# Attention in pairs of slots, with one batch of value products per pair, and maxima split before they are turned

## The chip, the cores and the metric

The kernel runs on one core of one Trainium2 chip. The time is that of the device in microseconds, from launch to end on that core. The kernel before took 1920.18 us in the median of three runs (1919.38 to 1920.65). The profiled execution is one further run.

## The reference

One pre-norm layer over x of 2 x 2048 tokens by 256: attention with 16 heads of 16 channels, then a feed-forward block with ternary weights.

```python
q, k, v = proj(Wq, bq), proj(Wk, bk), proj(Wv, bv)        # of layernorm(x)
scores = einsum('bhqd,bhkd->bhqk', q, k) / sqrt(16)
dp = clip(decay_params, 0.01, 0.9999)
mask = sum over 2 decays of softmax(mix_weights) * dp ** abs(t_q - t_k)
probs = softmax(scores * mask, axis=-1)                   # 2048 x 2048 for each batch and head
x = x + (probs @ v) @ Wo.T + bo
x = x + relu(layernorm(x) @ Wq1.T + b1) @ Wq2.T + b2      # Wq1, Wq2 are ternary: -1, 0, 1
```

No part of the 2048 x 2048 scores is skipped, and the maximum of each row is taken exactly, before the exponentials.

## The kernel before

Three blocks run one after another: a token block (norm, projections, tables of decay powers), the attention block, which is most of the time, and the feed-forward block. The change is in the attention block alone.

**Steps, units, slots.** The attention block makes 16 steps (8 pairs of heads in 2 batches). A step has two heads and 32 slots. Eight slots are a unit: one head and one half (1024) of its queries, so there are four units in a step. A slot handles two blocks of 128 keys. For each of them TensorE makes a tile of scores of 128 keys by 1024 queries (`scores`, L1054 to L1073), ScalarE makes its exponentials (L936), and TensorE multiplies them with the values into the bank `acc` (`products`, L1075 to L1089).

**Levels.** The decay is handled by levels: q and k come multiplied with powers of the decay for blocks of 1024, 512, 256 and 128, each as a sum of two fp16 parts (`hi`, `lo`), stacked in `q_stack` and `k_stack`. The block on the diagonal is taken from the raw q and k (the fifth level) times a mask. In half of the slots of a unit each tile has one such diagonal block, added by a transpose (L1066), in the other half none: "slots with a diagonal" and "slots without" below.

**Maxima.** A softmax needs the maximum of a row before its exponentials. So 12 slots ahead (`LEAD`) TensorE makes the scores once more, of 128 queries by 2048 keys (`max_scores`, L1018 to L1044). They pass through `ring`, three PSUM banks of 512 columns, in four items to a slot. VectorE reduces the items 0, 1 and 2 (L963), and of item 3 first 384 columns (L965) and then the 128 of the diagonal with the mask (L967). TensorE may write an item once VectorE has given back the bank that was filled three items earlier (`ring_free`). After a unit's last block VectorE reduces the parts to `row_max` (L976), ScalarE repeats it (L916), TensorE turns it into the ring (`turn_max`, L1052), VectorE splits it into two fp16 rows (L985, L987, L990), and SyncE stores these into `q_stack` (L776), whence they enter the next unit's scores as two more rows.

**Building the next pair.** During step i GpSimd multiplies q and k of the next pair with the powers (L157), ScalarE casts the product to `hi` (L165), and GpSimd subtracts for `lo` (L171), in 10 chunks (`CHUNKS`). Chunks 0 and 1 are the raw level, straight from `qk`. `cast` of chunk 0 waits for `qk_in` (the loads of `builder.load`, six DMAs) and for `raw_in` of both heads (the copies of the raw level of the build before, which read `hi` and `lo`).

**What sets the order.** All orders are written out by hand, each engine does its own in turn, and semaphores join them. SyncE issues the DMAs in one fixed order with waits between: in the third unit of a step it waits for the split maxima (L776), then issues `builder.load` of the pair after next (L117, L119, four at L125), a mask (L770), the six raw copies of head 1 (L752), and a store. ScalarE's casts of the next pair stand at the slots in `hi_slot`, chunk 0 at slot 0 of the step.

## Time and profile before

| | before |
|---|---|
| median of three runs | 1920.18 us |
| profiled execution | 1918.94 us |
| its span, first to last instruction | 1917.1 us |
| TensorE busy | 1795.7 us (94%) |
| VectorE busy | 1589.5 us (83%) |
| ScalarE busy | 1326.7 us (69%) |
| GpSimd busy | 812.1 us (42%) |
| mean granted TensorE clock | 0.969 |

An engine's instructions overlap their neighbours by their pipelines, so "busy" counts more than what an instruction holds up: the distance from one start to the next is what the argument uses. A granted clock of 1.00 is 2.4 GHz, 0.50 is 1.2 GHz. Times in a row are from the start of the span.

### The profile page before, as it was taken

The page shows a single profiled execution, that of the slowest core. Times are in us where ns is not written, and L with a number is a line of the kernel's source. Part 1 is how long each engine was busy: PE and PEld are TensorE (multiplying, and loading weights), DVE is VectorE, ACT ScalarE, POOL GpSimd, SP SyncE. Part 2 cuts the span into 40 slices and gives each one's busy share as a digit, 9 for nine tenths or more (in the row PEclk, how much of TensorE's full clock was granted, in tenths as well). Part 3 has the DMA queues.
Part 4 walks back from the last instruction along what each step waited for, and adds up shares of the span by engine and source line. Part 5 has one row for each costly group of instructions (what it writes and reads, how often), then busy time and mean ns, then how long its engine had stood idle before and what let it go on. Part 6 is the DMA issues. An engine that isn't in the chain of part 4 may idle for free. (4 is left out here: it accounts for less than half of the span.)

```text
span 1917.1 us, 32073 instructions
## 1 busy us (share of the span) xinstructions
PE 1795.7 (94%) x11794; PEld 749.4 (39%) x11794; DVE 1589.5 (83%) x3756; ACT 1326.7 (69%) x1526; POOL 812.1 (42%) x409
## 2 busy tenths in 40 slices
PE   3856999999999999999999999999999999995998
PEld 2521333333333333333333333333333333324666
DVE  7866888888888888888888888888888888835785
ACT  2343868686868686868686868686868686673555
POOL 6340908081818181818181818171727272002010
PEclk9875999999999999999999999999999999996999
DMA  6988363636363636363636363636363634207531
GB/s 156 267 270 192 75 154 91 154 90 155 91 155 90 154 91 154 94 154 94 154 94 154 93 154 94 154 94 153 93 154 93 154 94 110 67 18 187 146 91 34
DMA packets 132442, 242.62 MB, mean 127 GB/s; under 512 B 27696, under 2 KB 62896, under 8 KB 122032
## 3 DMA queue, kind: packets, MB, share of 16 engines
q1 hardware_dynamic: 129376, 237.84, 51.1%
q0 software_dynamic: 560, 2.36, 1.2%
q8 instruction: 92, 1.51, 0.3%
q10 hardware_dynamic: 2352, 0.40, 0.1%
q14 instruction: 62, 0.51, 0.1%
HBM read 69.08 MB, written 44.56 MB: 59 GB/s over the span
## 5 line engine op out<-in xcount | busy, mean ns | idle before, releaser
L936 ACT ACTIVATE probs<-tile 128x1024 f32<-128x1024 f32 x1024 | 999.5, 1024 | 297.8 <-PE tile L1066 170.0
L963 DVE TENSOR_REDUCE part_max<-ring 128x1 f32<-128x512 f32 x1536 | 964.0, 682 | 183.2 <-PE ring L1038 183.2
L1038 PE MATMUL ring<-k_stack,q_stack 96*128 96x512 f16 (+2 forms) x3072 | 661.1, 314 | 27.6 <-DMA q_stack<-lo 18.0
L1069 PE MATMUL tile<-q_stack,k_stack 98*128 98x512 f16 (+2 forms) x2560 | 588.6, 328 | 9.5 <-ACT probs L936 9.1
L1085 PE MATMUL acc<-probs,v_ones 128*32 128x512 f32 x4096 | 546.1, 605 | 0.0
L1069 PEld LDWEIGHTS tile<-q_stack,k_stack 98*128 98x128 f16 x2560 | 211.3, 98 | 575.5 <-ACT probs L936 346.7
L873 POOL TENSOR_TENSOR diag<-diag,row_max 128x1024 f32<-128x1024 f32 x64 | 121.4, 1897 | 643.1 <-DVE row_max L976 643.1
L1038 PEld LDWEIGHTS ring<-k_stack,q_stack 96*128 96x128 f16 x3072 | 262.6, 99 | 312.7 <-DVE part_max L963 178.9
L157 POOL TENSOR_TENSOR decayed<-qk,table_in 128x1024 f32<-128x1024 f32 x128 | 305.3, 2391 | 59.7 <-DMA table_in<-table_scratch 46.8
L965 DVE TENSOR_REDUCE part_max<-ring 128x1 f32<-128x384 f32 x512 | 278.8, 545 | 7.5 <-PE ring L1038 7.5
L171 POOL TENSOR_TENSOR lo<-decayed,hi 128x1024 f16<-128x1024 f32 x120 | 256.3, 2136 | 10.1 <-ACT hi L165 10.1
L165 ACT CAST hi<-decayed 128x1024 f16<-128x1024 f32 x128 | 134.3, 1049 | 61.1 <-POOL decayed L157 61.0
L967 DVE CUSTOM_DVE_ANT_0 diag<-ring,mask 128x128 f32<-128x128 f32 x512 | 143.3, 280 | 2.0
L1066 PE MATMUL tile<-ident,diag 128*128 128x128 f32 x512 | 142.8, 279 | 0.0
L171 POOL TENSOR_TENSOR lo<-qk,hi 128x1024 f16<-128x1024 f32 x30 | 64.1, 2137 | 178.2 <-ACT hi L165 178.2
L1085 PEld LDWEIGHTS acc<-probs,v_ones 128*32 128x32 f32 x4096 | 80.8, 108 | 57.0 <-issue 3.0
L1323 ACT ACTIVATE h_hi<-up,b_col 128x512 f16<-128x512 f32 x64 | 43.9, 685 | 54.4 <-PE up L1470 53.8
L1398 DVE TENSOR_TENSOR h_lo<-hidden,h_hi 128x512 f16<-128x512 f32 x64 | 50.1, 782 | 32.0 <-ACT hidden L1324 31.4
L1066 PEld LDWEIGHTS tile<-ident,diag 128*128 128x128 f32 x512 | 71.6, 140 | 6.2
L1284 POOL TENSOR_TENSOR x_bias<-x_res,bo_all 128x1024 f32<-128x1024 f32 x8 | 18.8, 2349 | 119.8 <-DVE y L1367 103.5
L927 ACT COPY heads_out<-acc 128x512 f32<-128x512 f32 x64 | 37.5, 586 | 22.3 <-PE acc L1085 22.3
L567 PE MATMUL turn<-ident,x_tokens 128*128 128x128 f32 x64 | 10.5, 318 | 39.3 <-DVE x_tokens L79 39.3
(145 smaller groups left out, 1041.1 us busy)
## 6 DMA issues: line engine op xcount, KB each, us to landing
q_stack<-hi SPq DMA_DIRECT2D x320, 128.0 KB, 3.8
k_stack<-hi SPq DMA_DIRECT2D x128, 256.0 KB, 4.3
q_stack<-lo SPq DMA_DIRECT2D x160, 128.0 KB, 3.0
table_in<-table_scratch SPq DMA_DIRECT2D x64, 256.0 KB, 8.3
k_stack<-lo SPq DMA_DIRECT2D x64, 256.0 KB, 3.7
out_scratch<-heads_out SPq DMA_DIRECT2D x64, 256.0 KB, 3.1
v_scratch<-v_out SPq DMA_DIRECT2D x8, 1024.0 KB, 6.5
q_scratch<-q_out SPq DMA_DIRECT2D x32, 256.0 KB, 3.8
```

Of the source, the lines that this page charges most:

```text
L157: self.nc.gpsimd.tensor_tensor(self.source(c), self.half_view(self.qk[:], level, side), self.factors(level, side), ALU.mult).then_inc(self ...
L165: self.nc.scalar.copy(self.half_view(self.hi[:, level], level, side), self.source(c)).then_inc(self.hi_ready, 1)
L171: ops.tensor_tensor(self.half_view(self.lo[:, level], level, side), self.source(c), self.half_view(self.hi[:, level], level, side), ALU.su ...
L873: nc.gpsimd.tensor_tensor(part, part, row_max[:, half].unsqueeze(2).broadcast_to([P, UNIT_SLOTS, P]), ALU.subtract).then_inc(diag_ready, 1)
L936: nc.scalar.activation(probs[:, t % 4], tile[t % 2][:].rearrange("p a b -> p (a b)"), ACT.Exp, scale=1.0 / (SCALE * SCALE * HEAD_DIM ** 0. ...
L963: nc.vector.tensor_reduce(out[:, k:k + 1], ring_bank(n), AX.X, ALU.max).then_inc(ring_free, 1)
L965: nc.vector.tensor_reduce(out[:, 3:4], ring_bank(n)[:, 0:3 * P], AX.X, ALU.max).then_inc(blocks_seen, 1)
L967: nc.vector.tensor_tensor_reduce(out=diag[h][:, q], in0=ring_bank(n)[:, 3 * P:4 * P], in1=mask[h][:], scale=1.0, scalar=-3.0e38, op0=ALU.m ...
L1038: last = nc.tensor.matmul(ring[:, n % RING, col:col + width], q_stack[h][0:STACK, q // UNIT_SLOTS, level, q0:q0 + P], k_stack[h][0:STACK, ...
L1066: last = nc.tensor.matmul(out, diag[h][:, kb], ident[:], is_transpose=True, start=bank not in started, stop=True, skip_group_check=True)
L1069: last = nc.tensor.matmul(out, k_stack[h][:, level, kb * P:(kb + 1) * P], q_stack[h][:, half, level, col:col + width], start=bank not in s ...
L1085: last = nc.tensor.matmul(acc[row:row + ROWS], v_ones[h][:, t % BLOCKS], probs[:, t % 4, qt * 512:(qt + 1) * 512], start=(j % UNIT_SLOTS = ...
```

## The change

- **Pairs of slots.** TensorE goes through slots two by two. The eight products (two slots' tiles) stand together at the end of the pair, after all scores and ring items of both; before, four stood at the end of each slot, for the tiles of the slot before. Item 0 of the ring comes ahead of the pair's first scores.
- **Maxima.** VectorE splits the maxima into two fp16 parts while they are 8 columns wide (`max_parts`); ScalarE repeats both; TensorE turns them by a matmul with the fp16 identity after the products of the pair of slots 4 and 5; VectorE copies them once (`take_max`). `finish_max` comes at slot 3 of a unit instead of slot 4. SyncE waits for `ring_free` of that item.
- **Casts.** One cast to a pair of slots, behind its four exponentials. Chunks 0 and 1 (raw) of the build after next are cast already at slots 25 and 27 of the step, and GpSimd's `begin` does the first four of its steps at the end of the step. SyncE's order of DMAs is the same.
- The copy of `acc` (`take_unit`) stands ahead of the unit's first exponential instead of behind the second.

```diff
@@ -625,7 +625,7 @@
-RED_SLOT, TURN_SLOT = 4, 5
+RED_SLOT, TURN_SLOT = 3, 5
...
+def turn_taken(slot, more, o):
+
+    return RING_STEP * o + turn_item(slot, more) + AHEAD_ITEMS + 1
 
 
...
+        max_parts = sb("max_parts", [P, MAXROWS, UNIT_SLOTS], F16)
+        max_repeated = sb("max_repeated", [P, MAXROWS, RAW, UNIT_SLOTS], F16)
         max_rows = sb("max_rows", [MAXROWS * RAW * UNIT_SLOTS, P], F16)
-        scrap = sb("scrap", [UNIT_SLOTS, 1])
...
-        order = [("rest", 0), ("rest", 1), ("product", 2)]
-        for c in range(3, CHUNKS):
+        order = [("rest", 2)]
+        for c in range(4, CHUNKS):
             order += [("product", c), ("rest", c - 1)]
         order.append(("rest", CHUNKS - 1))
-        pool_steps = (order[:5], order[5:14], order[14:], [])
-        hi_slot = (0, 1, 3, 4, 6, 7, 9, 10, 13, 15)
+        pool_steps = (order[:3], order[3:11], order[11:], [])
+        cast_slot = {2 * c - 3: c for c in range(2, CHUNKS)}
+        raw_slot = {SLOTS - 7: 0, SLOTS - 5: 1}
 
         @block.sync
...
-            def store_max_rows(h, half, count):
-
-                sp.wait_ge(rows_ready, count)
+            def store_max_rows(h, half, taken):
+
+                sp.wait_ge(ring_free, taken)
                 sp.dma_start(q_stack[h][STACK:STACK + MAXROWS, half, 0:RAW],
                              max_rows[:]).then_inc(rows_in, QUADS)
...
-                store_max_rows(1, 1, UNITS * i + 4)
+                store_max_rows(1, 1, turn_taken(2 * UNIT_SLOTS + TURN_SLOT, more, o))
...
+            def begin(builds):
+                for c in range(2):
+                    builder.rest(pool, nc.gpsimd, c, builds)
+                for c in range(2, 4):
+                    free(c, builds)
+                    builder.multiply(c)
+
             pool.sem_inc(diag_ready, 1)
             diag_minus_max(0, 0, 1)
+            begin(1)
             def step(i, o, more):
...
                     diag_minus_max((u // 2) % 2, u % 2, UNITS * i + u + 1)
+                if i + 2 < STEPS:
+                    begin(i + 2)
 
             for_steps(step)
...
 
-            def repeat_max(par, count):
-
-                act.wait_ge(max_ready, count)
-                nc.scalar.copy(max_repeated[:], row_max[:, par].unsqueeze(1).broadcast_to([P, MAXROWS * RAW, UNIT_SLOTS])
+            def repeat_max(count):
+
+                act.wait_ge(parts_ready, count)
+                nc.scalar.copy(max_repeated[:], max_parts[:].unsqueeze(2).broadcast_to([P, MAXROWS, RAW, UNIT_SLOTS])
                                ).then_inc(repeated_ready, 1)
 
 
...
+                    if s % UNIT_SLOTS == 0 and (s > 0 or o > 0):
+                        take_unit(s // UNIT_SLOTS - 1)
                     act.wait_ge(probs_used, SLOTS * o + s + 1)
                     for t in (2 * s, 2 * s + 1):
-                        u = s // UNIT_SLOTS + 1
-                        if s % UNIT_SLOTS == TURN_SLOT and t % 2 and (more or u < UNITS):
-                            repeat_max(u % 2, UNITS * i + u + 1)
                         act.wait_ge(tile_full, EXPS * o + t + 1)
                         nc.scalar.activation(probs[:, t % 4], tile[t % 2][:].rearrange("p a b -> p (a b)"), ACT.Exp,
                                              scale=1.0 / (SCALE * SCALE * HEAD_DIM ** 0.5)).then_inc(exp_done, 1)
-                    if s % UNIT_SLOTS == 0 and (s > 0 or o > 0):
-                        take_unit(s // UNIT_SLOTS - 1)
-                    for c in range(CHUNKS):
-                        if more and hi_slot[c] == s:
-                            cast(c, i + 1)
+                    if more and s in cast_slot:
+                        cast(cast_slot[s], i + 1)
+                    if i + 2 < STEPS and s in raw_slot:
+                        cast(raw_slot[s], i + 2)
+                    u = s // UNIT_SLOTS + 1
+                    if s % UNIT_SLOTS == RED_SLOT and (more or u < UNITS):
+                        repeat_max(UNITS * i + u + 1)
                 if o == STEPS - 1:
                     take_unit(UNITS - 1)
...
 
-            def finish_max(par, seen, count):
-
-                dve.wait_ge(blocks_seen, seen)
-                if count is not None:
-                    dve.wait_ge(diag_ready, count)
+            def finish_max(par, slot, unit, o=0):
+
+                dve.wait_ge(ring_free, RING_STEP * o + ring_item(slot, ITEMS - 1) + AHEAD_ITEMS + 1)
+                if unit >= 1:
+                    dve.wait_ge(diag_ready, unit)
                 nc.vector.tensor_reduce(row_max[:, par], part_max[:, par], AX.X, ALU.max).then_inc(max_ready, 1)
-
-            def split_max(slot, unit_count, more=True, o=0):
+                dve.wait_ge(max_ready, unit + 1)
+                if unit >= 1:
+                    dve.wait_ge(repeated_ready, unit)
+                nc.vector.tensor_scalar(max_parts[:, 0], row_max[:, par], -1.0 / MAXUNIT, None, ALU.mult
+                                        ).then_inc(high_ready, 1)
+                dve.wait_ge(high_ready, unit + 1)
+                nc.vector.scalar_tensor_tensor(out=max_parts[:, 1], in0=row_max[:, par], scalar=-1.0 / MAXUNIT,
+                                               in1=max_parts[:, 0], op0=ALU.mult,
+                                               op1=ALU.subtract).then_inc(parts_ready, 1)
+
+            def take_max(slot, unit_count, more=True, o=0):
 
                 n = turn_item(slot, more)
                 dve.wait_ge(ring_full, RING_STEP * o + n + AHEAD_ITEMS + 1)
                 if unit_count is not None:
                     dve.wait_ge(rows_in, QUADS * unit_count)
-                src = ring_bank(n)[0:MAXROWS * LO_ROWS, 0:P]
-                nc.vector.tensor_scalar(max_rows[:], src, -1.0 / MAXUNIT, None, ALU.mult).then_inc(max_seen, 1)
-                dve.wait_ge(max_seen, (unit_count if unit_count is not None else 0) + 1)
-                nc.vector.scalar_tensor_tensor(out=max_rows[LO_ROWS:], in0=src[LO_ROWS:], scalar=-1.0 / MAXUNIT,
-                                               in1=max_rows[LO_ROWS:], op0=ALU.mult,
-                                               op1=ALU.subtract).then_inc(rows_ready, 1)
-                nc.vector.tensor_copy(scrap[:], src[0:UNIT_SLOTS, 0:1]).then_inc(ring_free, 1)
+                nc.vector.tensor_copy(max_rows[:], ring_bank(n)[0:MAXROWS * LO_ROWS, 0:P]).then_inc(ring_free, 1)
 
             nc.vector.memset(unit[:], MAXUNIT).then_inc(unit_ready, 1)
             for s in range(-LEAD, 0):
                 max_block(s, s + LEAD, 0)
...
-                nc.tensor.transpose(ring[0:MAXROWS * LO_ROWS, n % RING, 0:P],
-                                    max_repeated[:].rearrange("p r b -> p (r b)"), ident[:]).then_inc(ring_full, 1)
+                nc.tensor.matmul(ring[0:MAXROWS * LO_ROWS, n % RING, 0:P], max_repeated[:].rearrange("p m r b -> p (m r b)"),
+                                 keep["ident16"][:], start=True, stop=True, skip_group_check=True).then_inc(ring_full, 1)
 
...
                 max_scores(s, s + LEAD, range(ITEMS), 0)
-                if s % UNIT_SLOTS == TURN_SLOT and s + LEAD >= UNIT_SLOTS:
+                if s == TURN_SLOT - UNIT_SLOTS:
                     turn_max(s, 1)
             pe.wait_ge(const_ready, 2)
             def step(i, o, more):
-                for s in range(SLOTS):
-                    ahead = more or s + LEAD < SLOTS
+                def ahead(s, ks):
+                    if more or s + LEAD < SLOTS:
+                        max_scores(s, s + LEAD, ks, i, o)
+
+                for s in range(0, SLOTS, 2):
                     if s % UNIT_SLOTS == 0:
                         u = s // UNIT_SLOTS
                         pe.wait_ge(rows_in, QUADS * (UNITS * i + u + 1))
                         pe.wait_ge(diag_ready, UNITS * i + u + 2)
+                    ahead(s, (0,))
                     scores(2 * s, o)
-                    if ahead:
-                        max_scores(s, s + LEAD, (0, 1), i, o)
+                    ahead(s, (1,))
                     scores(2 * s + 1, o)
-                    if s == SLOTS - 1 and o == STEPS - 1:
-                        products(s - 1, o)
-                    if ahead:
-                        max_scores(s, s + LEAD, (2, 3), i, o)
-                    j = s if s == SLOTS - 1 and o == STEPS - 1 else s - 1
-                    if j < 0 and o > 0:
-                        products(SLOTS - 1, o - 1)
-                    if j >= 0:
-                        if j % UNIT_SLOTS == 0:
-                            pe.wait_ge(acc_free, UNITS * i + j // UNIT_SLOTS + 1)
-                        if j % (2 * UNIT_SLOTS) == 0:
-                            pe.wait_ge(v_in[j // (2 * UNIT_SLOTS)], QUADS * (i + 1))
-                        products(j, o)
-                    if s % UNIT_SLOTS == TURN_SLOT and (more or s + UNIT_SLOTS < SLOTS):
-                        turn_max(s, UNITS * i + s // UNIT_SLOTS + 2, more, o)
+                    ahead(s, (2, 3))
+                    scores(2 * s + 2, o)
+                    ahead(s + 1, (0, 1))
+                    scores(2 * s + 3, o)
+                    ahead(s + 1, (2, 3))
+                    if s % UNIT_SLOTS == 0:
+                        pe.wait_ge(acc_free, UNITS * i + s // UNIT_SLOTS + 1)
+                    if s % (2 * UNIT_SLOTS) == 0:
+                        pe.wait_ge(v_in[s // (2 * UNIT_SLOTS)], QUADS * (i + 1))
+                    products(s, o)
+                    products(s + 1, o)
+                    if s % UNIT_SLOTS == TURN_SLOT - 1 and (more or s + UNIT_SLOTS < SLOTS):
+                        turn_max(s + 1, UNITS * i + s // UNIT_SLOTS + 2, more, o)
 
             for_steps(step)
```

On TensorE, slots without a diagonal in the first step, before: `tile` are scores of the tile that is exponentiated, `ring` the items for the maxima, `acc` the products with the values.

```order
L1069 MATMUL tile<-q_stack,k_stack 128x512 x2
L1038 MATMUL ring<-k_stack,q_stack 128x512 x2
L1069 MATMUL tile<-q_stack,k_stack 128x512 x2
L1038 MATMUL ring<-k_stack,q_stack 128x512
L1038 MATMUL ring<-k_stack,q_stack 128x256
L1038 MATMUL ring<-k_stack,q_stack 128x128 x2
L1085 MATMUL acc<-probs,v_ones 32x512 x4
L1069 MATMUL tile<-q_stack,k_stack 128x512 x2
L1038 MATMUL ring<-k_stack,q_stack 128x512 x2
L1069 MATMUL tile<-q_stack,k_stack 128x512 x2
```

The same slots after; ahead of the first row stand the eight products of the pair before, one `ring` item, two `tile` rows and one `ring` item.

```order
L1088 MATMUL tile<-q_stack,k_stack 128x512 x2
L1057 MATMUL ring<-k_stack,q_stack 128x512
L1057 MATMUL ring<-k_stack,q_stack 128x256
L1057 MATMUL ring<-k_stack,q_stack 128x128 x2
L1088 MATMUL tile<-q_stack,k_stack 128x512 x2
L1057 MATMUL ring<-k_stack,q_stack 128x512 x2
L1088 MATMUL tile<-q_stack,k_stack 128x512 x2
L1057 MATMUL ring<-k_stack,q_stack 128x512
L1057 MATMUL ring<-k_stack,q_stack 128x256
L1057 MATMUL ring<-k_stack,q_stack 128x128 x2
L1104 MATMUL acc<-probs,v_ones 32x512 x8
```

The products moved from behind every fourth ring item to behind every eighth.

On ScalarE, the start of the fourth unit of the first step (slots 24 to 27), before, from the copy of `acc` on, which here stands behind two exponentials:

```order
L927 COPY heads_out<-acc 128x512 [waits out_stored0,acc_full]
L936 ACTIVATE probs<-tile 128x1024 [waits tile_full,probs_used]
L936 ACTIVATE probs<-tile 128x1024 [waits tile_full]
L936 ACTIVATE probs<-tile 128x1024 [waits tile_full,probs_used]
L936 ACTIVATE probs<-tile 128x1024 [waits tile_full]
L936 ACTIVATE probs<-tile 128x1024 [waits tile_full,probs_used]
L936 ACTIVATE probs<-tile 128x1024 [waits tile_full]
```

The same place after:

```order
L946 COPY heads_out<-acc 128x512 [waits out_stored0,acc_full]
L954 ACTIVATE probs<-tile 128x1024 [waits tile_full,probs_used]
L954 ACTIVATE probs<-tile 128x1024 [waits tile_full]
L954 ACTIVATE probs<-tile 128x1024 [waits tile_full,probs_used]
L954 ACTIVATE probs<-tile 128x1024 [waits tile_full]
L165 CAST hi<-qk 128x1024 [waits raw_in1,raw_in0,qk_in]
L954 ACTIVATE probs<-tile 128x1024 [waits tile_full,probs_used]
L954 ACTIVATE probs<-tile 128x1024 [waits tile_full]
L954 ACTIVATE probs<-tile 128x1024 [waits tile_full,probs_used]
L954 ACTIVATE probs<-tile 128x1024 [waits tile_full]
L165 CAST hi<-qk 128x1024
```

Two casts that stood in the next step moved here, and the first waits for three semaphores of DMAs.

## Rows read from the trace of the kernel before

**Rows 1.** The stretches view of one whole step: engines' busy us, clock, DMA.

```profile
313.10:409.50 96.40, 95.76 (x646) 36.37 (x644) 84.76 (x208) 73.61 (x84) 47.41 (x23) 1.00 0.53 123
```

**Rows 2.** The timeline, ScalarE, one step apart: start us, us, engine, line.

```profile
313.08 0.58 ACT L927 COPY heads_out<-acc 128x512 f32<-128x512 f32 x1
...
409.46 0.59 ACT L927 COPY heads_out<-acc 128x512 f32<-128x512 f32 x1
```

**Rows 3.** The timeline, TensorE, two slots without a diagonal and one with.

```profile
797.13 0.60 PE L1069 MATMUL tile<-q_stack,k_stack 98*128 98x512 f16 x2
...
800.06 0.61 PE L1069 MATMUL tile<-q_stack,k_stack 98*128 98x512 f16 x2
800.50 0.60 PE L1038 MATMUL ring<-k_stack,q_stack 96*128 96x512 f16 x2
...
803.25 0.56 PE L1069 MATMUL tile<-q_stack,k_stack 98*128 98x512 f16 x3 [0.19 <-ACT probs L936]
...
805.24 1.07 PE L1085 MATMUL acc<-probs,v_ones 128*32 128x512 f32 x8
```

**Rows 4.** The same in narrow windows: rests of item 3, next scores, a turn.

```profile
801.67 0.40 PE L1038 MATMUL ring<-k_stack,q_stack 96*128 96x256 f16 x3
...
804.92 0.40 PE L1038 MATMUL ring<-k_stack,q_stack 96*128 96x256 f16 x3
...
806.24 0.50 PE L1069 MATMUL tile<-q_stack,k_stack 98*128 98x512 f16 x2
...
809.24 0.30 PE L1052 MATMUL ring<-ident,max_repeated 128*64 128x128 f32 x1
809.37 0.38 PE L1069 MATMUL tile<-q_stack,k_stack 98*128 98x512 f16 x1
```

**Rows 5.** TensorE in the last slots of the attention, products of two slots in turn.

```profile
1719.11 1.06 PE L1085 MATMUL acc<-probs,v_ones 128*32 128x512 f32 x8
...
1719.99 1.83 PE L1085 MATMUL acc<-probs,v_ones 128*32 128x512 f32 x8
```

**Rows 6.** The timeline, VectorE: one slot's four items, and a split.

```profile
800.92 1.89 DVE L963 TENSOR_REDUCE part_max<-ring 128x1 f32<-128x512 f32 x3 [0.37 <-PE ring L1038]
802.72 0.55 DVE L965 TENSOR_REDUCE part_max<-ring 128x1 f32<-128x384 f32 x1
803.19 0.28 DVE L967 CUSTOM_DVE_ANT_0 diag<-ring,mask 128x128 f32<-128x128 f32 x1
...
809.64 0.28 DVE L985 TENSOR_SCALAR max_rows<-ring 64x128 f16<-64x128 f32 x1
```

**Rows 7.** The timeline, ScalarE: a cast that waited, and four exponentials.

```profile
801.22 1.04 ACT L165 CAST hi<-decayed 128x1024 f16<-128x1024 f32 x1 [1.08 <-POOL decayed L157]
802.17 3.78 ACT L936 ACTIVATE probs<-tile 128x1024 f32<-128x1024 f32 x4
```

**Rows 8.** The timeline, SyncE: from the store of maxima to the last raw copy.

```profile
352.42 0.57 SPq L776 DMA_DIRECT2D q_stack<-max_rows  x1
...
360.70 0.59 SPq L752 DMA_DIRECT2D k_stack<-hi  x1
```

**Rows 9.** DMA issues (KB each, median us to landing), first 353.0 to 361.2, then 314 to 322.

```profile
k_stack<-hi SPq DMA_DIRECT2D x2, 128.0 KB, 8.2
...
q_stack<-hi SPq DMA_DIRECT2D x2, 128.0 KB, 2.4
```

**Rows 10.** The stretches view, TensorE alone: busy us (instructions), clock, DMA share, GB/s.

```profile
26.00:28.00 2.00, 0.48 (x5) 1.00 0.02 4
28.00:30.00 2.00, 0.00 (x0) 1.00 0.00 0
30.00:32.00 2.00, 1.52 (x10) 0.89 1.29 131
32.00:34.00 2.00, 2.00 (x6) 0.50 0.17 9
34.00:36.00 2.00, 2.00 (x9) 0.75 0.95 219
```

More of the change, by code:

```diff
@@ L705, in attention_block @@
         blocks_seen = sem("blocks_seen")
-        max_ready, max_seen = sem("max_ready"), sem("max_seen")
+        max_ready, high_ready, parts_ready = sem("max_ready"), sem("high_ready"), sem("parts_ready")
         repeated_ready = sem("repeated_ready")
-        rows_ready, rows_in = sem("rows_ready"), sem("rows_in")
+        rows_in = sem("rows_in")
         diag_ready = sem("diag_ready")
@@ L800, in _ @@
             builder.load(sp, 1)
-            store_max_rows(0, 0, 1)
+            store_max_rows(0, 0, turn_taken(TURN_SLOT - UNIT_SLOTS, True, 0))
             def step(i, o, more):
@@ L812, in step @@
                     store_out(i - 1, UNITS - 1)
-                store_max_rows(0, 1, UNITS * i + 2)
+                store_max_rows(0, 1, turn_taken(TURN_SLOT, more, o))
                 if more:
@@ L822, in step @@
                     load_q(0, 0, 0)
-                store_max_rows(1, 0, UNITS * i + 3)
+                store_max_rows(1, 0, turn_taken(UNIT_SLOTS + TURN_SLOT, more, o))
                 if more:
@@ L846, in step @@
                         load_q(1, 0, x)
-                    store_max_rows(0, 0, UNITS * i + 5)
+                    store_max_rows(0, 0, turn_taken(3 * UNIT_SLOTS + TURN_SLOT, more, o))
                 if o == STEPS - 1:
@@ L911, in _ @@
                                ).then_inc(const_ready, 1)
-            def repeat_max(par, count):
-                act.wait_ge(max_ready, count)
-                nc.scalar.copy(max_repeated[:], row_max[:, par].unsqueeze(1).broadcast_to([P, MAXROWS * RAW, UNIT_SLOTS])
+            def repeat_max(count):
+                act.wait_ge(parts_ready, count)
+                nc.scalar.copy(max_repeated[:], max_parts[:].unsqueeze(2).broadcast_to([P, MAXROWS, RAW, UNIT_SLOTS])
                                ).then_inc(repeated_ready, 1)
             nc.scalar.activation(warm[:], ident[:, 0:1], ACT.Exp)
-            repeat_max(0, 1)
+            repeat_max(1)
             act.sem_inc(exp_done, 2)
+            for c in range(2):
+                cast(c, 1)
             def step(i, o, more):
@@ L994, in _ @@
                 max_block(s, s + LEAD, 0)
-                if s % UNIT_SLOTS == RED_SLOT and s + LEAD >= UNIT_SLOTS:
-                    finish_max(0, s + LEAD + 1, None)
-                if s % UNIT_SLOTS == TURN_SLOT and s + LEAD >= UNIT_SLOTS:
-                    split_max(s, None)
+                if s == RED_SLOT - UNIT_SLOTS:
+                    finish_max(0, s, 0)
+                if s == TURN_SLOT - UNIT_SLOTS:
+                    take_max(s, None)
             def step(i, o, more):
@@ L1006, in step @@
                     if s % UNIT_SLOTS == RED_SLOT:
-                        seen = SLOTS * i + s + LEAD + 1
-                        if not more and s + LEAD >= SLOTS:
-                            dve.wait_ge(ring_free, RING_STEP * o + ring_item(SLOTS - LEAD - 1, ITEMS - 1) + AHEAD_ITEMS + 1)
-                            seen = SLOTS * STEPS
-                        finish_max(u % 2, seen, UNITS * i + u)
+                        finish_max(u % 2, s, UNITS * i + u, o)
                     if s % UNIT_SLOTS == TURN_SLOT:
-                        split_max(s, UNITS * i + u, more, o)
+                        take_max(s, UNITS * i + u, more, o)
             for_steps(step)
@@ L1096, in _ @@
                 max_scores(s, s + LEAD, range(ITEMS), 0)
-                if s % UNIT_SLOTS == TURN_SLOT and s + LEAD >= UNIT_SLOTS:
+                if s == TURN_SLOT - UNIT_SLOTS:
                     turn_max(s, 1)
```

1 line of the change is left out of this document (removed).

## The prediction

> **What bounds the kernel now.** I looked first at the busy times of one whole step [rows 1]: TensorE 95.8 of 96.4 us, VectorE 84.8, ScalarE 73.6, at the full clock. A step is 409.46 - 313.08 = 96.4 us [rows 2], and the 16 of them are 1542 of the 1917 us. Then TensorE's timeline: a slot without a diagonal takes 800.06 - 797.13 = 2.93 us, one with a diagonal 806.24 - 803.25 = 2.99 [rows 3, 4]. Sixteen of each make 94.7; four turns at 809.37 - 809.24 = 0.13 [rows 4] make 0.5; the other 1.2 us come from casts that wait for GpSimd and hold ScalarE up: the slot that begins at 800.06 takes 3.19 instead of 2.93 [rows 3], since a cast sat waiting in it [rows 7]. So TensorE is the bound, and the reader should see in VectorE's rows that it is close behind: the three reduces of a slot start 0.60 apart (802.72 - 800.92 for three), item 3 costs 0.47 + 0.28, together 2.55 us, and then it idles 0.37 [rows 6].
>
> **What the merged batch removes.** Going into the products costs time: item 3's last 512 columns start at 804.92 and the products at 805.24, 0.32 us [rows 3, 4], where 512 columns take 0.22 (1024 took 800.50 - 800.06 = 0.44) [rows 3]; 0.10 is the way in. Coming out costs too: eight product records last 806.24 - 805.24 = 1.00 us when scores follow [rows 3, 4], but 1719.99 - 1719.11 = 0.88 when products follow [rows 5]; 0.12 is the way out. One way in and out less per pair is 0.22 us, times 256 pairs 56 us. If TensorE stayed the bound, this would be the gain, and more (rivals).
>
> **What it adds: VectorE starves at each batch.** The ring has three banks. The last item 3 of a pair needs the bank of that slot's item 0. VectorE begins the three reduces at 800.92 and ends the first at 801.52, and TensorE starts item 3 at 801.67 [rows 4, 6]: 0.15 from VectorE's end to TensorE's start. From that start: 0.32 to the products, 0.88 + 1.00 for the batch, then item 0 of the next pair, which VectorE can read 0.42 after it starts (800.50 to 800.92) [rows 3, 6]. That is 2.62, plus the 0.15 before it 2.77 us, in which VectorE has the items 1, 2 and 3 left: 0.60 + 0.60 + 0.75 = 1.95. It idles 0.8 us per pair, whatever TensorE saves elsewhere, as long as item 3 is the one that waits. In the new order it is: single ring items lie between scores at the head of the pair, so VectorE also idles between items 0, 1 and 2. These start 0.22 + 0.44 = 0.66 apart without a diagonal and about 0.71 with one, where VectorE takes 0.60: 0.1 and 0.2 us per pair. VectorE's pair is then 2 x 2.55 + 0.8 + 0.1 or 0.2, 6.0 or 6.1 us, against TensorE's 5.86 and 5.98 before. The eight pairs of each kind make 8 x 12.1 = 97.0 us in a step. That the bound passes to VectorE is the whole price; the 56 us are spent in waiting for the ring.
>
> **Maxima.** The split now works on 8 columns: two small operations behind the row reduce, each with a wait for the one before. They lie at the end of the pair of slots 2 and 3, in VectorE's 0.8 us of idleness, and cost nothing; if that cover were gone, at most 0.6 us, twice the 0.28 of today's split, four times per step. The copy of 64x128 should take the 0.28 of the split of the same shape [rows 6]; it and the 0.13 of the turn fall at the head of a pair, partly over one another: 0.13 to 0.28, I take 0.2, four times per step 0.8. A step is 97.8 without the casts.
>
> **Casts 2 to 9.** They come behind a pair's four exponentials. ScalarE has 4 x 0.92 + 0.95 = 4.6 us [rows 7] of work in 6.0, and GpSimd begins earlier, so the 1.2 us of cast stalls go; that is already in the 97.8. So far: 97.8 - 96.4 = +1.4 us, times 16 steps +22 us (bounds: 0 and +45, by 0.1 us less or more per pair). GpSimd's four steps ahead and the copy of `acc` before the exponentials lie in idle time: GpSimd is busy 47 of 96 us, ScalarE 74 [rows 1].
>
> **The raw cast at slot 25.** This is the largest term. ScalarE works in order; the cast of chunk 0 there waits for DMAs that SyncE issues in the same unit. SyncE's order is unchanged: the last raw copy is issued 360.70 - 352.42 = 8.3 us after the store of the maxima and lands 8.2 us after that [rows 8, 9], so 16.5 after the store. The store comes later now: the turn stands at the end of the pair of slots 20 and 21, and with 0.42 for VectorE to see it, 0.28 for the copy and about 0.05 it is issued 0.8 us into the pair of 22 and 23, that is 5.3 us before the products of that pair are done. The raw level is thus in 11.2 us into the pair of 24 and 25. ScalarE is through the copy of `acc` and four exponentials about 0.35 + 0.6 + 0.2 + 4 x 0.92 = 4.8 us into it. It waits 6.4 us, casts in 0.95, and the exponential that was due at 6.0 + 1.2 = 7.2 starts at 12.1: 5 us late. TensorE has two tiles and can fill the ring, then waits for that exponential; nothing after it is ahead of time, so all 5 us are lost. It happens in the 14 steps with a build after next: 70 us. By bounds, 3 and 6.5 us a step (raw level landing 2 us sooner or 1.5 later): 42 and 91.
>
> The Trainium skill ("DMA: Bandwidth & Descriptors", on the two cost components) fits a DMA's time as about 2.0 us fixed plus its bytes at 436 GB/s. By that fit, as an estimate, the raw copies would land some 2.3 us after issue and the wait would be half a us. The same copy does land in 2.4 us where the queue is empty [rows 9]. Behind the six loads of the builder it took 8.2, so the trace speaks against the fit here; that it might hold is rival B.
>
> **The clock.** TensorE stands still about 5 us in each of these waits. In the token block it stood 0.48 us busy in 26 to 28, then not at all to about 30.5, 4.0 us; thereafter the granted clock was 0.89, 0.50 and 0.75 in three stretches of 2 us, which is 0.4 + 2.0 + 1.0 = 3.4 us at 1.2 GHz [rows 10]. Half of that is lost where TensorE is the bound: 1.7 us, times 14 = 24 us (bounds 0 and 35).
>
> The Trainium skill ("TensorE: Matmul & The Clock Gate", Part 1) holds that the cost of ramping is below 1% of a typical kernel's span; taken as an estimate, that is at most 19 us here where my term is 24, and the sum would be 2030.
>
> **The sum.** 1918.9 of the profiled execution (0.07% under the median of 1920.2) + 22 + 70 + 24 = 2035 us.
>
> **Rivals.** A: all as above, but the clock stays up, since items of the ring still run now and then in the wait: 2011. For it: the wait is interrupted by two tiles' scores at its start; against: the row above.
> B: the raw level is there when slot 25's exponentials end. Then the cast fits ScalarE's idle time: 1918.9 + 22 = 1941. Against: [rows 9] and SyncE's fixed order.
> C, the other side: VectorE doesn't starve and TensorE remains the bound. The pair would be 2 x 2.93 - 0.22 less the 0.08 per slot that item 3 waits now (item 3 starts at 801.67, where 800.50 + 0.44 + 0.44 + 0.22 = 801.60 was open to it), 5.48, and with a diagonal 5.98 - 0.22 - 0.04 = 5.72; a step 8 x 11.2 + 0.5 = 90.1 us, 6.3 less, 100 us in all: 1819. It decides from VectorE's idle time at a batch below 0.3 us instead of 0.8, which needs a ring that is given back sooner than rows 4 and 6 show. With the raw cast's wait of 5.6 us as well (78, and 24 for the clock) it is 1819 + 78 + 24 = 1921: the same.
> D: only part of the raw cast's wait reaches TensorE (half): 1918.9 + 22 + 35 + 12 = 1988.
>
> **How the numbers follow.** Forecast 0.57, A 0.17, B 0.09, D 0.08, C without the cast's wait 0.04, with it 0.03, anything else slower 0.02. Forecast's own range by the terms' bounds: 2005 to 2060. For 8 in 10 the range holds the forecast, A and the upper part of D: 1992 to 2058. A measurement of this kernel tells 0.2% (4 us) from no change: faster 0.04, same 0.03, slower 0.93.
>
> **What would show it.** Right: in the timeline products x16 records per pair and pairs 6.0 and 6.1 us long; VectorE idle 0.8 us before the first reduce of each pair; TensorE's weight loads waiting for `part_max` more than today; on ScalarE an idle time of some 6 us before the cast of `qk` at slot 25, ended by a DMA to a stack or `qk`; steps of 104 to 105 us in the first 14 and 98 in the last ones; a clock of 0.5 for about 3 us after each wait. Wrong: steps all alike (B); pairs under 5.8 us (C); a clock of 1.00 through the waits (A). The forecast falls if the store of the maxima in the third unit comes several us earlier than I placed it, or if the loads of the builder land sooner.

## The result and the profile after

The changed kernel takes 2224.8 us (median of four runs, 2223.8 to 2227.4), the kernel before 1920.4 in the same comparison: a ratio of 1.159 (95% interval 1.157 to 1.160). The forecast of 2035 had the sign right and missed 190 of the 304 us; its range ended at 2058.

The first rows of the page after (busy us, share of the span, instructions) tell where not to look. TensorE and VectorE are "busy" longer than before, on as many instructions, and yet by a smaller share of the span: both wait.

```profile
span 2223.8 us, 32136 instructions
PE 1903.8 (86%) x11794; PEld 826.8 (37%) x11794; DVE 1761.7 (79%) x3756; ACT 1322.6 (59%) x1526; POOL 812.3 (37%) x409
```

A step takes 113.9 to 118.3 us, mostly 116 (before 96.4 [rows 2], forecast 104 to 105). What the forecast had named is there. On ScalarE's timeline, the fourth unit of a step begins with the copy of `acc`; then come four exponentials, and the raw cast waits 6.25 us for a DMA (forecast 6.4). This place is one of the shorter of the 14: they range from 6.1 to 7.8 us, 6.9 in the mean.

```profile
977.17 0.59 ACT L946 COPY heads_out<-acc 128x512 f32<-128x512 f32 x1 [1.40 <-PE acc L1104]
977.93 3.77 ACT L954 ACTIVATE probs<-tile 128x1024 f32<-128x1024 f32 x4 [0.17 <-PE tile L1088]
987.95 1.04 ACT L165 CAST hi<-qk 128x1024 f16<-128x1024 f32 x1 [6.25 <-DMA k_stack<-hi]
```

SyncE had stored the maxima 16.4 us before that cast, and issued the last raw copy 8.3 us after them, as in [rows 8]:

```profile
971.50 0.58 SPq L782 DMA_DIRECT2D q_stack<-max_rows  x1
...
979.80 0.60 SPq L758 DMA_DIRECT2D k_stack<-hi  x1
```

TensorE stands still for 5.1 us in it; over the 14 waits it is 5.0 to 6.7 us, 5.8 in the mean (forecast 5).

```profile
984.26 0.60 PE L1057 MATMUL ring<-k_stack,q_stack 96*128 96x512 f16 x4
989.98 1.04 PE L1088 MATMUL tile<-q_stack,k_stack 98*128 98x512 f16 x2 [5.12 <-ACT probs L954]
```

The stretches view of TensorE there (length, busy us and instructions, granted clock, DMA share, GB/s) answers to [rows 10]: the clock goes to 1.2 GHz and is back at 2.4 by 996, so that some 6 us of work are done at half speed, against the 3.4 that the term had.

```profile
986.00:988.00 2.00, 0.00 (x0) 1.00 1.01 288
988.00:990.00 2.00, 0.02 (x1) 0.79 1.09 244
990.00:992.00 2.00, 2.00 (x5) 0.50 0.39 79
992.00:994.00 2.00, 2.00 (x10) 0.50 0.00 0
994.00:996.00 2.00, 2.00 (x12) 0.50 0.04 8
996.00:998.00 2.00, 2.00 (x18) 1.00 0.00 0
```

The surprise is in the groups of instructions by form (busy us, mean ns of one, idle before): the two operations on 8 columns, costed at nothing, take 1.76 and 1.06 us in the mean. The reduce ahead of them, on 40 columns, takes 0.20.

```profile
L1003 DVE SCALAR_TENSOR_TENSOR max_parts<-row_max,max_parts 128x8 f16<-128x8 f32 x64 | 112.6, 1759 | 2.2
L1000 DVE TENSOR_SCALAR max_parts<-row_max 128x8 f16<-128x8 f32 x64 | 67.6, 1057 | 2.4 <-DVE row_max L996 0.2
...
L996 DVE TENSOR_REDUCE row_max<-part_max 128x8 f32<-128x40 f32 x64 | 12.5, 195 | 2.2
```

VectorE's timeline of one such place, in the second unit of a step (start, us):

```profile
904.99 0.20 DVE L996 TENSOR_REDUCE row_max<-part_max 128x8 f32<-128x40 f32 x1
905.22 1.98 DVE L1000 TENSOR_SCALAR max_parts<-row_max 128x8 f16<-128x8 f32 x1
907.23 1.81 DVE L1003 SCALAR_TENSOR_TENSOR max_parts<-row_max,max_parts 128x8 f16<-128x8 f32 x1
908.96 0.68 DVE L983 TENSOR_REDUCE part_max<-ring 128x1 f32<-128x512 f32 x1
```

And GpSimd's at the same time:

```profile
905.04 2.12 POOL L171 TENSOR_TENSOR lo<-decayed,hi 128x1024 f16<-128x1024 f32 x1 [0.29 <-ACT hi L165]
907.12 1.89 POOL L879 TENSOR_TENSOR diag<-diag,row_max 128x1024 f32<-128x1024 f32 x1
```

The reader should lay the ends beside each other. GpSimd's first instruction ends at 907.16, VectorE's first at 907.20; GpSimd's second at 909.01, VectorE's second at 909.04. VectorE's operation ends when GpSimd's has. TensorE then waits for a bank of the ring:

```profile
909.70 0.39 PE L1057 MATMUL ring<-k_stack,q_stack 96*128 96x256 f16 x3 [2.68 <-DVE part_max L983]
```

The second operation meets the subtraction `diag_minus_max` (L879), which the same reduce releases: 63 of the 64 begin inside a GpSimd instruction, take 1.75 to 1.82 us and end 0.02 to 0.03 us after it; the one that met none took 0.17. The first meets a build step of GpSimd in the second and third unit of a step: 31 of the 64 begin inside a GpSimd instruction (1.76 to 2.12 us), and the 33 others take 0.17. Over the whole trace TensorE's matmuls into the ring stand idle 96.7 us for VectorE's reduces; in the kernel before it was under 2 us.

### The profile page after: what moved, and what is told of

It is laid out like the page before. It is cut to its first block and busy times, and to the rows that moved or that the text cites. A ratio compares the mean times of both kernels' runs of the same rounds, so it can differ in the third digit from the quotient of the medians.

```text
span 2223.8 us, 32136 instructions
## 1 busy us (share of the span) xinstructions
PE 1903.8 (86%) x11794; PEld 826.8 (37%) x11794; DVE 1761.7 (79%) x3756; ACT 1322.6 (59%) x1526; POOL 812.3 (37%) x409
## 5 line engine op out<-in xcount | busy, mean ns | idle before, releaser
L983 DVE TENSOR_REDUCE part_max<-ring 128x1 f32<-128x512 f32 x1536 | 996.6, 685 | 228.5 <-PE ring L1057 220.8
L954 ACT ACTIVATE probs<-tile 128x1024 f32<-128x1024 f32 x1024 | 974.9, 1024 | 290.5 <-PE tile L1085 155.6
L1057 PE MATMUL ring<-k_stack,q_stack 96*128 96x512 f16 (+2 forms) x3072 | 753.7, 329 | 126.8 <-DVE part_max L983 96.7
L1088 PE MATMUL tile<-q_stack,k_stack 98*128 98x512 f16 (+2 forms) x2560 | 619.6, 341 | 108.3 <-ACT probs L954 98.6
L1057 PEld LDWEIGHTS ring<-k_stack,q_stack 96*128 96x128 f16 x3072 | 292.7, 102 | 586.2 <-DVE part_max L983 236.9
L171 POOL TENSOR_TENSOR lo<-decayed,hi 128x1024 f16<-128x1024 f32 x120 | 255.2, 2127 | 419.3 <-ACT hi L165 419.1
L879 POOL TENSOR_TENSOR diag<-diag,row_max 128x1024 f32<-128x1024 f32 x64 | 121.3, 1895 | 707.0 <-DVE row_max L996 707.0
L157 POOL TENSOR_TENSOR decayed<-qk,table_in 128x1024 f32<-128x1024 f32 x128 | 304.5, 2385 | 59.4 <-DMA table_in<-table_scratch 47.7
L985 DVE TENSOR_REDUCE part_max<-ring 128x1 f32<-128x384 f32 x512 | 279.3, 546 | 7.4 <-PE ring L1057 7.4
L1104 PEld LDWEIGHTS acc<-probs,v_ones 128*32 128x32 f32 x4096 | 133.1, 115 | 191.0 <-issue 116.8
L932 ACT COPY max_repeated<-max_parts 128x64 f16<-128x64 f16 x64 | 15.6, 243 | 235.4 <-DVE max_parts L1003 235.4
L987 DVE CUSTOM_DVE_ANT_0 diag<-ring,mask 128x128 f32<-128x128 f32 x512 | 142.6, 278 | 0.0
L1003 DVE SCALAR_TENSOR_TENSOR max_parts<-row_max,max_parts 128x8 f16<-128x8 f32 x64 | 112.6, 1759 | 2.2
L165 ACT CAST hi<-qk 128x1024 f16<-128x1024 f32 x32 | 33.1, 1041 | 106.2 <-DMA k_stack<-hi 97.1
L1013 DVE CAST max_rows<-ring 64x128 f16<-64x128 f32 x64 | 18.1, 283 | 85.8 <-PE ring L1071 85.8
```

The lines of the kernel that those rows point to most:

```text
L157: self.nc.gpsimd.tensor_tensor(self.source(c), self.half_view(self.qk[:], level, side), self.factors(level, side), ALU.mult).then_inc(self ...
L165: self.nc.scalar.copy(self.half_view(self.hi[:, level], level, side), self.source(c)).then_inc(self.hi_ready, 1)
L171: ops.tensor_tensor(self.half_view(self.lo[:, level], level, side), self.source(c), self.half_view(self.hi[:, level], level, side), ALU.su ...
L879: nc.gpsimd.tensor_tensor(part, part, row_max[:, half].unsqueeze(2).broadcast_to([P, UNIT_SLOTS, P]), ALU.subtract).then_inc(diag_ready, 1)
L954: nc.scalar.activation(probs[:, t % 4], tile[t % 2][:].rearrange("p a b -> p (a b)"), ACT.Exp, scale=1.0 / (SCALE * SCALE * HEAD_DIM ** 0. ...
L983: nc.vector.tensor_reduce(out[:, k:k + 1], ring_bank(n), AX.X, ALU.max).then_inc(ring_free, 1)
```

## The experiments

The theory after the result, P: an operation of VectorE on SBUF that needs what GpSimd is holding is held until GpSimd's instruction ends; six held operations per step, 4 x 1.6 + 2 x 1.8 = 10 us of VectorE's time, are what the forecast lacks. The second operation is held in all four units of a step, the first in two. The rival, R: these operations are long but hidden, and the raw cast's wait and the clock cost more than forecast. Each ratio below is against the kernel before, with its 95% interval.

**Maxima split after the turn again.** `finish_max` is only the reduce, ScalarE repeats `row_max`, and VectorE splits the turned rows:

```diff
-                nc.vector.tensor_scalar(max_parts[:, 0], row_max[:, par], ...)       # and max_parts[:, 1]
-                nc.vector.tensor_copy(max_rows[:], ring_bank(n)[0:MAXROWS * LO_ROWS, 0:P])
+                nc.vector.tensor_scalar(max_rows[:], src, -1.0 / MAXUNIT, None, ALU.mult)      # src: the ring's bank
+                nc.vector.scalar_tensor_tensor(out=max_rows[LO_ROWS:], in0=src[LO_ROWS:], ...)
```

> The changed kernel with one part undone: the maxima are split as before, from the ring's bank after the turn, and nothing on VectorE but the row reduce stands behind the unit's last block. Theory P (VectorE's two operations on 8 columns in SBUF are held until GpSimd's running instruction ends, 1.76 to 2.0 us each instead of 0.17): six held operations per step go, 11 us; steps of 104 to 106 us in the first 14, total 2035 to 2080. Theory R (those operations are long but hidden, and the excess over the forecast comes from the raw cast's wait and the clock): within 30 us of the changed kernel's 2225.

Measured: 2066.6 us, 1.075 (1.073 to 1.076); steps of 105 to 108. 158 us are gone, 9.9 us per step, although three operations that read the ring's bank are back. TensorE's matmuls into the ring stand idle 13.7 us for VectorE instead of 96.7. R falls. The raw cast waits as in the changed kernel:

```profile
914.08 1.05 ACT L165 CAST hi<-qk 128x1024 f16<-128x1024 f32 x1 [6.21 <-DMA k_stack<-hi]
```

**Raw casts later.**

```diff
-        raw_slot = {SLOTS - 7: 0, SLOTS - 5: 1}
+        raw_slot = {SLOTS - 3: 0, SLOTS - 1: 1}
```

> The changed kernel with the casts of the raw chunks at slots 29 and 31 instead of 25 and 27. Theory P with the cast's wait as forecast (5 us lost and a clock drop of some 3 us of TensorE's time, in each of 14 steps): 2225 - 14 x 8 = 2113, up to 2140 if part of the clock's loss stays; steps of 108 to 109 us. Theory R' (the wait at slot 25 is hidden behind something else that is late there too): 2225 within 10 us.

Measured: 2128.4 us, 1.108 (1.106 to 1.110); steps of 109. ScalarE's timeline shows the cast without a wait:

```profile
950.73 1.05 ACT L165 CAST hi<-qk 128x1024 f16<-128x1024 f32 x1
```

96 us less, 6.9 per step of the 14: the wait and the clock after it. The last full step, in which no raw cast was left, takes 104.8 us here and 106.2 in the changed kernel.

**Both.**

> Both at once: maxima split as before, raw casts at slots 29 and 31; pairs of slots, the order of items and one cast per pair stay. This is the ring term alone: theory P with VectorE starved at each batch expects pairs of 6.0 and 6.1 us, steps of 97.7 to 99.5, 1940 to 1970. Theory C (TensorE stays the bound, one way in and out less per pair): steps near 90, about 1820.

Measured: 1959.1 us, 1.020 (1.018 to 1.021); steps of 98.1. What is left of the loss is the price of the pairs. TensorE's timeline shows a pair without a diagonal of 909.62 - 903.69 = 5.93 us; with a diagonal it is 6.06. The forecast had 6.0 and 6.1. The pair after a turn, one to a unit, takes 6.54: about 0.5 us more, where the forecast had 0.2.

```profile
903.69 1.92 PE L1101 MATMUL acc<-probs,v_ones 128*32 128x512 f32 x16
...
909.62 1.93 PE L1101 MATMUL acc<-probs,v_ones 128*32 128x512 f32 x16
```

VectorE, before the first reduce of the pair, idles the 0.80 us that the forecast worked out, where it had 0.37 per slot [rows 6]:

```profile
905.97 0.69 DVE L983 TENSOR_REDUCE part_max<-ring 128x1 f32<-128x512 f32 x1 [0.80 <-PE ring L1054]
```

**Products at the end of each slot again.** As the last one, but TensorE's loop is that of the kernel before, and `take_unit` stands behind the slot's exponentials:

```diff
-                for s in range(0, SLOTS, 2):          # pairs, products(s) and products(s + 1) at the end
+                for s in range(SLOTS):                # scores, items 0 and 1, scores, items 2 and 3, products(s - 1)
```

> As the one with both undone, and TensorE's order and ScalarE's place for the copy of acc are those of before too: four products at the end of each slot. Left of the change are the casts (one per pair behind the exponentials, raw chunks at slots 29 and 31 of the step before) and GpSimd's four steps ahead. If the merged batch costs time as forecast: 30 to 50 us less than the kernel with both undone, 1905 to 1915, a little under the kernel before. If the merged batch saves 56 us, this one is 50 us over it.

Measured: 1912.1 us, 0.996 (0.994 to 0.997); steps of 95.6. The order in pairs costs 47 us (1959.1 - 1912.1). That is more than the batch alone: here the products at a slot's end are those of the slot before, in the pairs they are the pair's own, and the ring's item 0 stands elsewhere; these parts were not undone one by one. What is left of the change gains 9 us on the kernel before. ScalarE's casts of the products waited 61.0 us in all for GpSimd there and 9.3 here, which fits GpSimd's early start; `finish_max` at slot 3 and the place of ScalarE's repeat moved too and are not separated from it.

**GpSimd's subtraction after both parts.** In the changed kernel:

```diff
             def diag_minus_max(h, half, count):
-                pool.wait_ge(max_ready, count)
+                pool.wait_ge(parts_ready, count)
```

> The changed kernel, but GpSimd's subtraction of the maxima waits for both parts (parts_ready) instead of the row maxima (max_ready), so that it can't run beside VectorE's second operation on 8 columns. Theory P (an operation of VectorE that needs the way into SBUF which GpSimd holds is held until GpSimd's instruction ends): the second operation takes 0.17 us in all 64 units instead of 1.76 to 1.82; the first still takes about 2.0 in the second and third unit of a step, where a build step of GpSimd runs. 4 x 1.6 = 6.4 us less per step and less loss by the clock: 2225 - 102 = 2122, down to 2080. Rival (a chained operation with fp16 output on 8 columns takes 1.8 us whatever GpSimd does): the second stays at 1.8, the time at 2225 or slightly above.

Measured: 2087.6 us, 1.087 (1.086 to 1.089). One wait on GpSimd moved, not an instruction of VectorE touched, and VectorE's second operation takes 0.17 us in all 64 units. The first, with GpSimd building in the second and third unit, is still held 30 times, 1.97 to 2.12 us. These cost little by themselves: the kernel is 21 us above the one that splits after the turn. TensorE's matmuls into the ring stand idle 30.8 us for VectorE, a third of the 96.7. VectorE's timeline, first and second unit of a step:

```profile
823.24 0.17 DVE L1000 TENSOR_SCALAR max_parts<-row_max 128x8 f16<-128x8 f32 x1
823.44 0.17 DVE L1003 SCALAR_TENSOR_TENSOR max_parts<-row_max,max_parts 128x8 f16<-128x8 f32 x1
...
848.60 1.98 DVE L1000 TENSOR_SCALAR max_parts<-row_max 128x8 f16<-128x8 f32 x1
850.61 0.17 DVE L1003 SCALAR_TENSOR_TENSOR max_parts<-row_max,max_parts 128x8 f16<-128x8 f32 x1
```

**The operations by themselves, on the kernel before.** Two are added behind the row reduce, and nobody reads what they write:

```diff
+                dve.wait_ge(max_ready, ...)
+                nc.vector.scalar_tensor_tensor(out=probe[:, 0], in0=row_max[:, par], scalar=-1.0 / MAXUNIT, in1=row_max[:, par], ...)
+                dve.wait_ge(probe_seen, ...)
+                nc.vector.scalar_tensor_tensor(out=probe[:, 1], in0=row_max[:, par], scalar=-1.0 / MAXUNIT, in1=row_max[:, par], ...)
```

> The kernel before with two operations added behind each unit's row reduce on VectorE, chained by semaphores, on 8 columns of SBUF with two inputs from SBUF and fp16 output, whose result nobody reads. Theory P: the second always meets GpSimd's subtraction of the maxima and takes about 1.8 us, the first takes 0.17 or up to 2.1 as GpSimd is free or in a build step; 1.5 to 3 us more per unit on TensorE's path after VectorE's spare 0.4 us per slot is used: 1980 to 2100. If nothing holds them: 0.17 each, 1921 to 1935.

Measured: 2050.2 us, 1.067 (1.066 to 1.069). Two operations on 8 columns, 64 times, cost the kernel 130 us. All 64 of the second are held; of the first 49 take 0.17 us, and 15 begin inside a GpSimd instruction and take 0.2 to 1.4. The view of the second's line (ns, least, median, most):

```profile
L982 DVE SCALAR_TENSOR_TENSOR probe<-row_max x64: 1758/1761/1821, 183.0 to 1827.3; 128x8 f16<-128x8 f32 x64
```

The timeline of one place shows the order of starts that decides, first VectorE:

```profile
701.45 0.17 DVE L979 SCALAR_TENSOR_TENSOR probe<-row_max 128x8 f16<-128x8 f32 x1
701.65 1.76 DVE L982 SCALAR_TENSOR_TENSOR probe<-row_max 128x8 f16<-128x8 f32 x1
```

and GpSimd:

```profile
701.49 1.90 POOL L874 TENSOR_TENSOR diag<-diag,row_max 128x1024 f32<-128x1024 f32 x1 [23.49 <-DVE row_max L977]
```

The first began 0.04 us before GpSimd and was not held; the second began inside GpSimd's 1.90 us and ended with them (701.65 + 1.76 = 703.41, 701.49 + 1.90 = 703.39).

**The same with reduces.**

```diff
+                nc.vector.tensor_reduce(probe[:, 0], row_max[:, par].unsqueeze(2), AX.X, ALU.max)      # and probe[:, 1]
```

> The same with two reduces in place of the two operations: as many columns, the same place and the same chain of semaphores, but one input. Theory P with the way into SBUF as the cause: not held, 0.1 to 0.2 us each, the time 1921 to 1935. Rival (anything that VectorE writes to or reads from SBUF while GpSimd runs is held): as the run with two inputs, 1980 to 2100.

Measured: 1921.4 us, 1.000 (0.999 to 1.001). As many columns, the same output type, the same chain of waits beside the same GpSimd instruction, and nothing is held:

```profile
L981 DVE TENSOR_REDUCE probe<-row_max x64: 160/161/163, 183.7 to 1697.8; 128x8 f16<-128x8 f32 x64
```

So it is not that VectorE touches SBUF beside GpSimd, nor the size, nor the wait. The kind of operation alone isn't it either: in the kernel before the same two kinds, `tensor_scalar` and `scalar_tensor_tensor`, read the ring's bank in PSUM (L985, L987); 30 of the 64 of each began inside a GpSimd instruction and took 0.28 us like the others. Held were those two kinds with all their inputs in SBUF.

**A better kernel.** From the version with products at each slot's end, with the pairs' idea of single ring items at the head:

```diff
+                    if ahead:
+                        max_scores(s, s + LEAD, (0,), i, o)
                     scores(2 * s, o)
                     if ahead:
-                        max_scores(s, s + LEAD, (0, 1), i, o)
+                        max_scores(s, s + LEAD, (1,), i, o)
```

> The kernel with products at the end of each slot, maxima split after the turn and raw casts at slots 29 and 31 (measured 1912), with one change: of the ring's items, 0 comes ahead of the slot's first scores and 1 between the two scores, as in the pairs, where both stood between. Item 3 waits for VectorE to give back item 0 by 0.08 us in slots without a diagonal; with item 0 some 0.44 us earlier that wait goes, and VectorE's idle time moves to the front of the slot. Expected: slots without a diagonal 2.85 us instead of 2.93, those with one slightly shorter too, steps of 94 to 95 us, 1880 to 1895, 1 to 2% under the kernel before. Rival (an exponential then waits longer for its tile and holds TensorE): 1912 or more.

Measured: 1882.6 us, 0.980 (0.979 to 0.982), faster than both kernels; steps of 93.75. A slot without a diagonal takes 2.84 us (before 2.93), one with a diagonal 903.11 - 900.14 = 2.97:

```profile
900.14 0.39 PE L1054 MATMUL ring<-k_stack,q_stack 96*128 96x512 f16 x1
...
902.11 1.07 PE L1101 MATMUL acc<-probs,v_ones 128*32 128x512 f32 x8
903.11 0.39 PE L1054 MATMUL ring<-k_stack,q_stack 96*128 96x512 f16 x1
```

Item 0 at the head of a slot is worth 29.5 us by itself (1912.1 - 1882.6). The pairs had it at their head already, so against the nearest order in slots they cost 76.5 us (1959.1 - 1882.6), not 47. VectorE waits 0.18 us where it waited 0.37 [rows 6]:

```profile
900.57 2.12 DVE L983 TENSOR_REDUCE part_max<-ring 128x1 f32<-128x512 f32 x3 [0.18 <-PE ring L1054]
```

## Why the prediction was wrong

**The step that failed** is this sentence: "They lie at the end of the pair of slots 2 and 3, in VectorE's 0.8 us of idleness, and cost nothing; if that cover were gone, at most 0.6 us". The two operations cost 158 us (changed kernel against the split after the turn) or 169 (the same with the raw casts late: 2128.4 - 1959.1). What the runs showed in its place: 1.76 us for the second and about 2.0 for the first where GpSimd runs, 10 us of VectorE's time per step against the 0.8 us of cover at one batch. The sum held nothing for it, and the bound of 0.6 four times per step would have been 38 us.

Their size was taken from an operation of the kernel before that read the ring's bank in PSUM [rows 6]; the bound of 0.6 went by it too. In the steps of the kernel before, VectorE had no scalar or two-input operation with all its inputs in SBUF, so no row there could warn. Ahead of the steps the same trace had both. In the token block a `tensor_scalar` on 4 columns of SBUF (L73) takes 0.17 us in five of its eight places and 0.28, 1.12 and 4.02 us in the three where it begins inside a GpSimd instruction, each time ending 0.03 us after it. The longest of them, VectorE and then GpSimd:

```profile
35.87 4.02 DVE L73 TENSOR_SCALAR rstd<-mv 128x4 f32<-128x4 f32 x1
34.40 5.46 POOL L368 TENSOR_SCALAR above<-w_rows,cut 128x2048 f16<-128x2048 f32 x1
```

The ends are 39.89 and 39.86. While the first pair is built, VectorE's subtraction of 1024 columns in SBUF (L171) takes 1.2 us in five places and 1.8 to 3.4 in the five where it begins inside a GpSimd instruction. With these rows the bound would have been GpSimd's own durations in the steps, 1.9 to 2.4 us (L873, L171, L157).

The Trainium skill ("SBUF — State Buffer", sections "SBUF: two separate sides" and "Who interferes with whom") has a rule: VectorE and GpSimd share one pair of ports by an exclusive lock. VectorE takes part for an operation in a two-port mode or, against a GpSimd instruction that reads SBUF, for one with two SBUF inputs; whoever starts first has the pair for its whole instruction, and the other blocks. The runs agree with it where VectorE came second: 1.76 us beside an instruction of 1.90, 2.0 beside one of 2.12, 0.16 for a reduce with one input, 0.28 for the operations that read PSUM. Where VectorE's operation on 8 columns came first, GpSimd's 1.90 us show no delay, the same as alone; behind one of 1024 columns it lost about 1 us (the last section). The same page of the Trainium skill says that `tensor_scalar` can enter a two-port mode. That would be why the scalar operation with its single fp32 input is held (L1000); no run here shows the mode.

**Casts, the wait at slot 25:** right as a mechanism, a little too small. Forecast 6.4 us on ScalarE and 5 on TensorE, measured 6.9 and 5.8 in the mean of the 14. With the clock the term was 94 us; it measured 96 beside held maxima and 107.5 without (2066.6 - 1959.1). In the kernel without held maxima TensorE's 14 stands make 79 us of that (5.7 each, forecast 70), so as an estimate 28 are left for the clock (forecast 24). **The clock:** the mechanism right. Some 6 us of work ran at 1.2 GHz after the wait, for 3.4; half of it would be 3 us a time, and 2 are left by the estimate, so the term came near its size with two parts off, which is in part luck. The clock also falls after the stands that the held operations cause: the mean granted clock was 0.916 in the changed kernel, 0.948 without the held operations, 0.969 without the raw wait as well.

**The ring:** right as a mechanism, 0.8 us of idleness and pairs of 5.93 and 6.06 where 6.0 and 6.1 stood. The term was +22 us and measured 38 (1959.1 - 1921.0). Steps account for 29.5 of it. The rest was left out: in the last step, where no ring items remain for most slots, the last three units take 69.9 us instead of 60.4. The batch is of the pair's own tiles, so TensorE has to wait for ScalarE's four exponentials before it, and ScalarE for TensorE's next scores behind it, 1.80 us in each pair there:

```profile
1751.09 3.79 ACT L954 ACTIVATE probs<-tile 128x1024 f32<-128x1024 f32 x4 [1.80 <-PE tile L1082]
```

**The saving that was to be eaten** (the way in and out of a batch, 56 us) was not measured by itself; that VectorE's period replaces it is shown by the 0.80 us. **Rivals:** B is excluded by the wait at slot 25, C by the pairs of 5.93 us and the 1959 us of the kernel with both undone, A by the clock, D by the 5.8 us of the wait's 6.9 that reach TensorE. None of them held the mechanism that mattered.

**The sum as it stands.** Without the held operations the kernel takes 2066.6 us, 32 above the forecast: 16 us are the ring's term, 13.5 the raw wait with its clock, and 2 the kernel before, which took 1921.0 in that comparison. The range of 2005 to 2060 is called that of the terms' bounds; all lower bounds together make 1961 and all upper ones 2090. The eight pairs of each kind make 96.8 us, not 97.0.

The parts add up, each from one kernel to the next: held operations 158, raw wait and clock 107.5, merged batch 47, casts and GpSimd's early start -9; together 304, as measured. The term that was missing is about half of the loss. They can't be read as independent: the raw wait costs 96 or 107 by what else is late.

## What to carry to other kernels

Making an operation smaller is no gain if it moves from PSUM to SBUF beside a busy GpSimd: VectorE's scalar and two-input operations there took what was left of GpSimd's instruction, on 8 columns as on 4. Search the whole trace for an operation of the same kind and place before costing it, also outside the block that changes. Before such an operation is added, look at what GpSimd runs at that moment, above all what the same event releases on it; let GpSimd start after it, as one changed wait did here for 137 us. Where a ring of banks feeds an engine, compare how long the producer's batch lasts with the work that the ring holds: here 2.77 us against 1.95, and the difference was lost; a deeper ring was not tried. A cast or copy that waits for loads belongs where the last load has landed, not where its engine is idle.

## What the runs showed of the hardware

- VectorE's `scalar_tensor_tensor` with two SBUF inputs and `tensor_scalar` with one, on 8 columns: 0.17 us with GpSimd idle, and until 0.02 to 0.03 us after GpSimd's end where they began inside one of its instructions (0.2 to 2.12 us). `tensor_reduce` on 8 and on 40 columns: 0.16 and 0.20 us in either case. A VectorE operation that had begun 0.04 us before GpSimd's was not held.
- It goes the other way too: in the kernel before GpSimd's product (L157), 2.35 us alone, took 3.27 to 3.39 us the three times that VectorE's subtraction of 1024 SBUF columns (L171, 1.2 us) had begun 0.05 to 0.15 us ahead of it.
- Reads of PSUM by the same two operations with output to SBUF (64 and 32 rows of 128 columns) took 0.28 us in the kernel before, in the 30 of 64 places beside GpSimd as in the others. The copy that the change puts in their place (L1013) kept 0.27 to 0.28 us in all 64 cases; 42 began inside a GpSimd instruction.
- After a stand of 5.1 us TensorE worked some 6 us at 1.2 GHz before it was back at 2.4; after a stand of 2.68 us, in the changed kernel, the granted clock was 0.91, 0.50 and 0.73 in the three stretches of 2 us from 909 us on.
